# Per-slot softmax scaling replaced by one combine per group of four, and one buffer in place of two for the query weights

## The reference

```python
x = x + attn(layernorm(x))          # causal softmax attention, wq wk wv wo
x = x + ffn(layernorm(x))           # (silu(x @ w_gate.T) * (x @ w_up.T)) @ w_down.T

scores = einsum('bhqd,bhkd->bhqk', q, k) / sqrt(128)   # causal mask, then
attn   = softmax(scores, axis=-1)
out    = einsum('bhqk,bhkd->bhqd', attn, v)
```

## Time and profile before

| | |
|---|---|
| median of 2 runs | 3052.99 us (3036.2 to 3069.78) |
| profiled execution | 3058.75 us, of which the slowest core's span is 3056.8 us |
| spans of the 8 cores | 3018.3 to 3056.8 us |
| busy in the span: TensorE, VectorE, ScalarE | 2520.3, 590.7, 552.9 us |

### The profile page before, as it was taken

One profiled execution on the slowest core, in us unless ns is written; L12 is line 12 of the kernel. 1 busy time (PEld: TensorE's weight loads), 2 busy tenths in 40 slices (PEclk: granted clock), 3 DMA queues, 4 the chain that ended last, 5 costly groups with the idle time before them and its releaser, 6 DMA issues.

```text
span 3056.8 us, 32132 instructions; the slowest of 8 cores (3018.3 to 3056.8 us)
## 1 busy us (share of the span) xinstructions
PE 2520.3 (82%) x12111; PEld 1173.0 (38%) x12352; DVE 590.7 (19%) x1186; ACT 552.9 (18%) x1090; POOL 169.2 (6%) x324
## 2 busy tenths in 40 slices
PE   1667888778777777775887999999999999797976
PEld 1323333333333333332333444444444444343433
DVE  4322222332322332231331010101010100000000
ACT  4333222322322232222231000000000000000000
POOL 0000000000000000000000000000000001111110
PEclk9877878998988998996888999999999999898988
DMA  6433200100100100004324444444444444555554
GB/s 183 110 86 73 35 14 14 21 14 15 21 15 14 21 15 15 14 8 98 110 109 84 76 77 78 78 77 77 76 76 76 76 69 70 110 76 110 75 110 92
DMA packets 61494, 196.38 MB, mean 64 GB/s; under 512 B 6944, under 2 KB 6944, under 8 KB 56096
## 3 DMA queue, kind: packets, MB, share of 16 engines
q0 software_dynamic: 46080, 134.24, 26.9%
q1 hardware_dynamic: 15264, 60.07, 6.0%
HBM read 311.72 MB, written 16.78 MB: 107 GB/s over the span
## 4 chain that ended last, share of the span: by engine, by line
PE 77%; ACT 6%; DVE 6%; issue 6%; DMA 4%; DVEq 0%; SPq 0%; ACTq 0%; POOL 0%; POOLq 0%
PE psA L735 7%; PE psB L746 7%; PE psA L397 5%; PE psA L417 4%; PE psB L397 4%; PE psF L746 4%; PE psD L735 4%; PE psB L417 4%; PE psA L820 4%; PE psB L820 4%; PE psE L746 3%; PE psC L735 3%; ACT p_sb L463 3%; PE psA L333 2%; PE psB L333 2%
## 5 line engine op out<-in xcount | busy, mean ns | idle before, releaser
L463 ACT ACTIVATE p_sb<-psA,stats 128x1024 bf16<-128x1024 f32 (+3 forms) x128 | 132.3, 1033 | 683.8 <-PE psA L446 396.5
L735 PE MATMUL psA<-h_fm,wg 128*128 128x512 bf16 x1004 | 226.8, 381 | 9.3 <-issue 8.3
L746 PE MATMUL psB<-h_fm,wu 128*128 128x512 bf16 x1004 | 225.0, 379 | 1.1
L746 PE MATMUL psF<-h_fm,wu 128*128 128x512 bf16 x512 | 194.0, 379 | 1.1
L735 PE MATMUL psD<-h_fm,wg 128*128 128x512 bf16 x512 | 194.0, 379 | 1.1
L735 PE MATMUL psC<-h_fm,wg 128*128 128x512 bf16 x491 | 186.1, 379 | 0.0
L746 PE MATMUL psE<-h_fm,wu 128*128 128x512 bf16 x491 | 186.1, 379 | 0.0
L820 PE MATMUL psB<-wd,hidden 128*128 128x512 bf16 x502 | 153.2, 384 | 20.9 <-DVE osb L834 20.3
L820 PE MATMUL psA<-wd,hidden 128*128 128x512 bf16 x501 | 152.4, 383 | 6.1 <-DVE osb L834 3.8
L735 PEld LDWEIGHTS psA<-h_fm,wg 128*128 128x128 bf16 x1024 | 100.3, 98 | 130.6 <-issue 10.9
L397 PE MATMUL psA<-h_fm,wkbuf 128*128 128x512 bf16 x502 | 140.3, 445 | 11.5 <-ACT p_sb L463 9.6
(11 more groups left out here) (124 smaller groups left out, 3052.0 us busy)
## 6 DMA issues: line engine op xcount, KB each, us to landing
wg<-wg_t POOLq DMA_DIRECT2D x64, 512.0 KB, 5.0
wu<-wu_t POOLq DMA_DIRECT2D x64, 512.0 KB, 5.0
wd<-wd_t POOLq DMA_DIRECT2D x128, 256.0 KB, 3.8
xt<-xkv SPq DMA_DIRECT2D x16, 1024.0 KB, 5.8
wqbuf<-wq_t POOLq DMA_DIRECT2D x16, 512.0 KB, 6.2
xt<-xq SPq DMA_DIRECT2D x8, 1024.0 KB, 11.0
wkbuf<-wk_t POOLq DMA_DIRECT2D x16, 512.0 KB, 5.1
wvbuf<-wv_t POOLq DMA_DIRECT2D x16, 512.0 KB, 5.3
```

The source lines that it names most:

```text
L463: t_exp = P.do("scalar", lambda e, s=s, slo=slo, shi=shi, sec=sec, sc_t=sc_t, sstat=sstat: e.activation(sb["p_sb"][:, P_OFF[s] + slo:P_OFF ...
L735: t_gmm = P.do("tensor", lambda e, hc=hc, c=c, half=half, par=par, gb=gb: e.matmul(bk(gb[half]), wg[par][:, c, :], sb["h2_fm"][:, c, half ...
L746: t_umm = P.do("tensor", lambda e, hc=hc, c=c, half=half, par=par, ub=ub: e.matmul(bk(ub[half]), wu[par][:, c, :], sb["h2_fm"][:, c, half ...
```

## The change

There are three edits. (1) `wqbuf2` goes: all query weight tiles pass through `wqbuf`, so the load of head `h` waits for the matmuls of head `h-1`; the wait of `emit_wv_dma` for `wqbuf2` goes too. (2) The three VectorE instructions per slot go from `emit_scores_softmax`; `emit_combine` is called once behind slots 0 to 3 and once behind slots 4 to 7. (3) The `drain(99)` behind slots 0 to 3 is moved behind `emit_k`.

```diff
@@ emit_q_head
-        qb = sb["wqbuf"] if h % 2 == 0 else sb["wqbuf2"]
-        t_w = P.dma("gpsimd", lambda e, h=h, qb=qb: e.dma_start(
-            out=qb[:, :, :], in_=dr["wq"][h, :, :, :]),
-            [qbuf_free[h % 2]], "wld")
+        t_w = P.dma("gpsimd", lambda e, h=h: e.dma_start(
+            out=sb["wqbuf"][:, :, :], in_=dr["wq"][h, :, :, :]),
+            [qbuf_free], "wld")
...
-        qbuf_free[h % 2] = P.tok("pe")
+        qbuf_free = P.tok("pe")
@@ emit_wv_dma
-            [vbuf_free, qbuf_free[1]], "wld")
+            [vbuf_free], "wld")
@@ emit_scores_softmax
         nsec = (nch + 1) // 2
-        grp_exp[g] = []
...
         exp_tok[s] = grp_exp[g][-1]
-        st_t = sb["stats"]
-        rcol = st_t[:, C_RG + s:C_RG + s + 1]
-        if nsec == 2:
-            t_sg = P.do("vector", lambda e, s=s, sstat=sstat, rcol=rcol: e.tensor_reduce(
-                rcol, sstat[:, 48 + s * 2:50 + s * 2], AXX, AOP.add),
-                waits=grp_exp[g][-2:] + [slot_free[s]], inc="dve")
-        else:
-            t_sg = P.do("vector", lambda e, s=s, sstat=sstat, rcol=rcol: e.tensor_copy(
-                rcol, sstat[:, 48 + s * 2:49 + s * 2]),
-                waits=[exp_tok[s], slot_free[s]], inc="dve")
-        t_rc = P.do("vector", lambda e, rcol=rcol: e.reciprocal(rcol, rcol),
-                    waits=[t_sg], inc="dve")
-        diag_tok[s] = P.do("vector", lambda e, s=s, rcol=rcol: e.tensor_scalar(
-            sb["diag"][:, s, 0, :], eye[:, :], rcol, None, AOP.mult),
-            waits=[t_rc, t_eye, diag_free[s]], inc="dve")
-        slot_free[s] = diag_tok[s]
@@ loop over the heads
         for i, s in enumerate((0, 1, 2, 3)):
             emit_scores_softmax(h, s)
             drain(3)
-        drain(99)
+        emit_combine(h, 0)
         if h + 1 < NH:
             emit_wk_dma(h + 1)
             emit_k(h + 1)
+        drain(99)
         pend = tpv_steps(h, 0, [0, 1, 2, 3])
         for i, s in enumerate((4, 5, 6, 7)):
             emit_scores_softmax(h, s)
             drain(5)
+        emit_combine(h, 1)
         if h + 1 < NH:
             emit_wv_dma(h + 1)
             emit_v(h + 1)
```

More of the change, by code:

```diff
@@ L51 @@
     "wqbuf":  (201344, [128, NKT, 128], BF16),
-    "wqbuf2": (224896, [128, NKT, 128], BF16),
     "o_fm":   (115328,  [128, NH, QR], BF16),
@@ L318, in emit_program @@
     ab_free = {"A0": None, "A1": None, "B0": None, "B1": None}
-    qbuf_free = [None, None]
+    qbuf_free = None
     def emit_q_head(h):
         nonlocal qbuf_free
-        qb = sb["wqbuf"] if h % 2 == 0 else sb["wqbuf2"]
-        t_w = P.dma("gpsimd", lambda e, h=h, qb=qb: e.dma_start(
-            out=qb[:, :, :], in_=dr["wq"][h, :, :, :]),
-            [qbuf_free[h % 2]], "wld")
+        t_w = P.dma("gpsimd", lambda e, h=h: e.dma_start(
+            out=sb["wqbuf"][:, :, :], in_=dr["wq"][h, :, :, :]),
+            [qbuf_free], "wld")
         banks = ("A0", "A1") if (h % 2 == 0) else ("B0", "B1")
@@ L332, in emit_q_head @@
                 w = [t_w, t_h1q_done, ab_free[bank]] if c == 0 else []
-                t_mm = P.do("tensor", lambda e, h=h, sp=sp, c=c, bank=bank, qb=qb: e.matmul(
-                    bk(bank), qb[:, c, :],
+                t_mm = P.do("tensor", lambda e, h=h, sp=sp, c=c, bank=bank: e.matmul(
+                    bk(bank), sb["wqbuf"][:, c, :],
                     sb["h1q"][:, c, sp * 512:(sp + 1) * 512],
@@ L372, in emit_program @@
     grp_free = [None, None]
-    slot_free = [None] * NQ
     grp_exp = [[], []]
```

## The result

The changed kernel takes 2909.54 us (median of 11 runs, 2899.3 to 2945.13), the kernel before 3050.53 us (median of 10). The ratio is 0.954, 95% interval 0.9507 to 0.9573: 4.6% faster, some 141 us. Forecast were 2956 us and a gain of 97, with a range that began at 2912.

The account below looks back on a forecast made before the run. TensorE, busy 82%, was taken as the bound, idling 118.5 us behind VectorE's evictions. Profiled execution: 3058.75 - 103.6 + 5.4 + 1.6 = 2962.1 us; the same 96.6 us off the 3052.99 median gives 2956, range 2912 to 2998.

Parts of the forecast that it names:

- What bounds: Attention's score phases: TensorE idles 118.5 us in 104 places for VectorE's evictions, queued behind instructions that wait for exponentials.
- The walk: One head's slots timed without the three instructions: 3.87 us saved in slots 4 to 7, 2.78 in 0 to 2; together 103.6.
- T(5) to T(7): Slot 5, between two odd steps: the second starts at 541.25 us instead of 542.76, saving 1.51 us.
- T(3) to T(9): Odd steps in slots 4 and 5: the first starts 0.57 us earlier, later ones keep 1.51 us.
- the exponential's bank: Slot 7: the value projection waits only for the bank slot 7's exponential reads, starting at 550.55 instead of 552.16; saved 1.61.
- the 59 to 61 given as a sign: Attention heads: taking about 59 to 61 us each would show the forecast right.
- The combine's price: Behind each group's last exponential: about 1.6 us, hidden under the projection except in the last head; +1.6 us.
- The price of the loads: Query stage with one buffer: load time beyond 5.9 us of cover costs 5.4 us over 15 loads, bounds 0 to 18.
- The clock: Attention: denser score phases might shift heads between clock levels, 36 us up or down; taken as 0.
- ScalarE took over: Rival in slots 4, 5 and 2: waits for ScalarE's evictions replace those for VectorE's; about 3002 us, chance 0.07.
- The clock went up, not down: Rival in attention: denser work lowers the clock and 82 us come back; 3038 us, chance 0.05.
- The others: Remaining rivals: combine uncovered by projections, 3007 us, 0.03; late query loads, 3167, 0.03; change does nothing, 3058, 0.02.

Follow-up runs that it names:

- e3: Changed kernel with the same three small VectorE instructions per slot behind each group instead of the combine; ratio to the kernel before 0.9601.
- e10: Changed kernel with each slot's three VectorE instructions of before, set behind the steps drained after that slot; ratio to the kernel before 0.961.
- e1: Kernel before with the combine alone, still two query weight buffers; ratio to the kernel before 0.9563.
- e2: Kernel before with one query weight buffer alone, the three VectorE instructions per slot kept; ratio to the kernel before 0.9976.
- e6: Kernel before with 34 unread matmuls per head set ahead of the longest waits for VectorE's eviction; ratio to the kernel before 0.9883.
- e4: Changed kernel with the three VectorE instructions at their old place in slots 4 to 7 only; ratio to the kernel before 0.981.
- e11: Changed kernel with the three VectorE instructions at their old place in slots 0 to 3 only, a repeat run; ratio to the kernel before 0.976.
- e12: e1 with each query load issued as late as with one buffer, both buffers kept; 2914.84 us profiled, kernel before 3055.4 to 3075.06 beside it.

## Why the prediction was right and where it failed

*What bounds.* Right. The evictions stood behind the exponentials, and e3 and e10 show that the place of the three instructions in the queue did it. The Trainium skill says of it that ScalarE's and VectorE's queues are strictly first in, first out (page "TensorE: Matmul & The Clock Gate", section on the array's architecture); the rows agree, with a ready eviction waiting behind the exponential TensorE stood idle for up to 2.7 us.

*The walk.* Right within a tenth in the sum. Slots 4 to 7: 3.87 us per head forecast, 67.8 / 15 = 4.5 measured on core 4. Slots 0 to 3: 2.78 forecast, 41.4 / 15 = 2.8 measured. All but about 10 us of the 109 is in the sum. The rest may be that I left slow matmuls at their slow rate inside slots 4 and 5: T(5) to T(7) took 1.33 us where the walk had 1.52. No run separates it. T(3) to T(9) came out in the order walked, and the value projection follows the exponential's bank as walked. A head takes mostly 56.6 to 58 us, less than the 59 to 61 given as a sign.

*The combine's price.* Right: beneath the projection, 2.2 us of waits for it in all, where 1.6 were set for the last head. The cover is gone there in two places and not one, since the last head has no key projection either. VectorE's busy time fell by 32.7 us, where 40 were estimated.

*Edit 3.* Nothing, as forecast; no experiment isolates it, but e1 and the changed kernel, which differ in it and in the buffer, agree.

*Edit 1.* The price of the loads was twice what they cost, and that the whole came out near it is luck: the slowest core starts attention 5.8 us later, but only 2.8 of these are the loads. From issue to first matmul the changed kernel's core 3 needs 5.9 to 6.4 us, and once 7.3; beyond the 6.0 of the earlier trace rows that sums to 2.8 us over 15 loads, where 5.4 was forecast. TensorE's row shows one wait for it (core 3):

```profile
PE psB L331 <- DMA wqbuf<-wq_t: 1.3, 1, 1.3
```

The kernel as a whole did not become slower (e2: 0.9976). In e2's trace six of the eight cores start attention at 317 to 322 us, since their granted clock in the query stage was 0.84 to 0.86. Giving up the second buffer cost nothing that can be seen here, as the earlier trace rows had it: the layernorm in front of each head covers the load.

*The clock: the step that failed.* "I take 0" for the clock, with 36 us either way. It was worth 44.7 us in the projections of the slowest core, and perhaps some of the 10 us that the walk missed in the score phases. Two terms are in it.

- 27.6 us are falls to 1.2 GHz in the first halves of the later projections. The rows for them were at hand: on the page of before the bank A groups, those that follow a score phase, lie at 445 and 418 ns beside bank B's 390 and 386. Their excess over 379 ns, 66 x 502 + 39 x 497 ns, is 52.5 us as an estimate, 12 of them in the first three heads. The text took the clock's sign as unknown. These falls followed the idle time that the change removes, as e6 shows by filling it, so at least for this idle time the sign could be told.
- 17.1 us are the first three heads, nearly all of it the 0.81 (15.8 us in e6, where the idle time is filled). The 0.78 in the first row is this 0.81, mixed with short falls to 1.2 GHz. The traces of e1 and e2 do not have it, and no experiment shows what brings it. That the changed kernel was spared it was not predictable from the rows, and this part of the miss is luck.

Core 3 of before lies 18.7 us above the changed kernel's core 3 in the projections, and core 4 lies 44.7 above: the slowest core is the one that the clock had hit hardest, and a change that evens it out gains the slowest core's loss, not the mean.

*The rivals.* ScalarE took over 21 us of waits, not the whole (73.7 to 94.7). The clock went up, not down, 0.89 to 0.99 over attention, and gate and up projection, with TensorE busy from 1500 to 2350 us without a gap, ran at 1.00. The others did not occur.

## What to carry to other kernels

On an engine with one in-order queue ask of each instruction that waits for something late what stands behind it that is ready; move the waiting one behind the ready ones before thinking of batching it. The same question then goes to the next engine: evictions behind ScalarE's exponentials were worth another 2%. And when idle time of TensorE goes, price the clock of the work that follows it as well, from the rows that compare the first matmuls after the gap with the later ones. Keep it apart from stretches in which the later ones are slow too: those the change may not touch.

## What the runs showed of the hardware that was not expected

More work made the kernel faster: e6's 544 added matmuls, in place of idle time, brought the projections of the later heads from up to 16.3 us on core 4 to 13.5 and the time down by 1.2%. The Trainium skill says that idle gaps of TensorE cost clock afterwards (page "TensorE: Matmul & The Clock Gate", section on oscillation). The rows agree for these projections, with gaps of at most 2.7 us each; the key projections of e4 and e11 do not follow from the gap right ahead.

TensorE's clock record has a third granted level beside 1.2 and 2.4 GHz, 0.81, at which a matmul of 512 columns takes 436 ns and a projection 16.4 us. In the traces of before, of the changed kernel and of e1, e2, e6 and e12 it comes in stretches of some 160 us, on both cores of a batch item at once. One stretch in the query stage makes a mean of about 0.76 there in place of about 0.85, worth 12 us; one at the start of attention makes the first three heads slow. No run here shows what brings it, and the denser gate and up projection runs without it.
